# Depthwise matrices and products in 101 instead of 112 lanes, ones in one lane, and two first loads of matrices at the MLP's strips 6 and 12

## The reference, cut to what matters

```python
h = jnp.einsum('oc,bchw->bohw', w1, x)              # 48 -> 288 channels
h = relu(bn(h, g1, b1, m1, v1))
h = conv3x3_depthwise(h, wd, padding=1)             # 288 groups
h = relu(bn(h, gd, bd, md, vd))
h = jnp.einsum('oc,bchw->bohw', w2, h)              # 288 -> 48 channels
return x + bn(h, g2, b2, m2, v2)
```

## Time and profile before

| what | us |
|---|---|
| median of three runs | 2052.09 (2045.63 to 2053.95) |
| the profiled execution's own time | 2046.83 |
| its span | 2044.9 |

### The profile page before, as it was taken

The page is one execution under the profiler, slowest core; times in us unless marked ns, Lnnn a source line. Parts: engine busy times, 40 slices in busy tenths (PEclk is TensorE's granted clock), DMA queues, the critical chain, the costliest instruction groups (busy, mean ns, idle before and its releaser), DMA issues.

```text
span 2044.9 us, 76366 instructions
## 1 busy us (share of the span) xinstructions
PE 1939.0 (95%) x29704; PEld 1598.8 (78%) x29704; DVE 1447.2 (71%) x2586; ACT 1369.1 (67%) x2838; POOL 648.0 (32%) x869
## 2 busy tenths in 40 slices
PE   6999999999999996799999999999999899999998
PEld 4888888888888884455555798888888898888987
DVE  5999999999999995455556556556556556565554
ACT  2787878877778874466666566656656566666655
POOL 4333333333333325013000432525234333425230
PEclk9999999999999997899999999999999999999999
DMA  2222222222222225666554435536263545455341
GB/s 65 72 75 71 75 75 73 75 75 75 75 75 75 75 68 124 150 141 157 136 135 111 102 82 137 100 90 150 72 128 95 114 106 117 87 136 102 98 99 33
DMA packets 286441, 199.46 MB, mean 98 GB/s; under 512 B 225991, under 2 KB 275672, under 8 KB 276488
## 3 DMA queue, kind: packets, MB, share of 16 engines
q1 hardware_dynamic: 282114, 189.12, 37.3%
q0 software_dynamic: 2368, 6.98, 1.9%
q10 hardware_dynamic: 1750, 0.39, 0.1%
HBM read 129.10 MB, written 54.72 MB: 90 GB/s over the span
## 4 chain that ended last, share of the span: by engine, by line
PE 56%; ACT 2%; DMA 1%; issue 1%; DVE 1%; ACTq 0%
PE psum L1091 13%; PE psum L1110 13%; PE psum L1136 10%; PE psum L670 6%; PE psum L655 6%; PE psum L1145 5%; PE psum L644 3%; ACT h2T L1191 1%; DMA room<-tok_mid 1%; DVE h L870 1%; ACT room L736 0%; DVE room L870 0%; ACT room L740 0%; ACTq L722 0%; DMA room<-in_fc_wT 0%
## 5 line engine op out<-in xcount | busy, mean ns | idle before, releaser
L919 POOL TENSOR_TENSOR mats<-mats,dscale 112x2048 f32<-112x2048 f32 x72 | 260.9, 3624 | 455.9 <-DMA mats<-in_taps 453.1
L1091 PE MATMUL psum<-ew,xp 64*100 64x96 f32 x6144 | 318.5, 252 | 24.0 <-DVE h L870 11.2
L1191 ACT ACTIVATE h2T<-psum 96x1024 f32<-96x1024 f32 x192 | 195.9, 1021 | 198.3 <-PE psum L1145 198.3
L870 DVE TENSOR_SCALAR h<-psum 100x384 f32<-100x384 f32 x384 | 212.1, 557 | 155.7 <-PE psum L1091 134.8
L1091 PEld LDWEIGHTS psum<-ew,xp 64*100 64x100 f32 x6144 | 291.3, 165 | 33.6 <-DVE h L870 14.1
L1110 PE MATMUL psum<-h,mats 112*64 112x128 f32 x4608 | 269.3, 276 | 6.6 <-issue 5.0
L1110 PEld LDWEIGHTS psum<-h,mats 112*64 112x64 f32 x4608 | 253.6, 138 | 15.5 <-issue 6.3
L869 ACT ACTIVATE room<-psum 64x512 f32<-64x512 f32 (+1 forms) x384 | 206.6, 538 | 84.6 <-PE psum L1110 78.1
L343 PE MATMUL psum<-kb,qa 128*64 128x256 f32 x2048 | 253.2, 383 | 1.0 <-DVE prob L437 0.5
L870 DVE TENSOR_SCALAR room<-psum 64x512 f32<-64x512 f32 (+1 forms) x288 | 174.2, 605 | 71.7 <-PE psum L1110 65.7
L1136 PE MATMUL psum<-h2T,pw 128*64 128x128 f32 x3072 | 211.1, 280 | 11.3 <-ACT h2T L1191 9.5
(11 more groups left out here) (152 smaller groups left out, 3245.9 us busy)
## 6 DMA issues: line engine op xcount, KB each, us to landing
mats<-in_taps SPq DMA_DIRECT2D x69, 896.0 KB, 6.7
tok_mid<-mid SPq DMA_DIRECT2D x128, 224.0 KB, 1.9
room<-tok_mid SPq DMA_DIRECT2D x64, 448.0 KB, 3.8
piece<-img_mid SPq DMA_DIRECT2D x196, 63.8 KB, 2.4
img_mid<-room SPq DMA_DIRECT2D x128, 97.5 KB, 2.9
kb<-kk SPq DMA_DIRECT2D x512, 24.0 KB
out<-yc SPq DMA_DIRECT2D x32, 384.0 KB, 4.5
scratch<-in_x_tokens SPq DMA_DIRECT2D x126, 96.0 KB, 2.0
```

Of the source, the lines that this page charges most:

```text
L870: return nc.vector.tensor_scalar(dst, src, 0.0, None, ALU.max)
L919: nc.gpsimd.tensor_tensor(m, m, bc(scale[0:MROWS, at:at + TCH], 2, POUT), ALU.mult).then_inc(mats_scaled, 1)
L1091: mm = nc.tensor.matmul(ring[(j + u) % 4][0:PIN, p:4 * CH:4], xp[hx][rows, 2 * j + p, :], w1[rows, c, :], start=True, stop=True)
L1191: nc.scalar.activation(h2T[n % 2][0:CH, :, :], turned_at(n, last)[0:CH, :, 0:POUT * PART], ACT.Copy).then_inc(copied, 1)
```

## The change

MROWS becomes PIN + 1 = 101: the matrices in DRAM, their loads, their scaling, the products of L1110 and the batch norm's tiles `dn` lose the lanes 101 to 111. The ones are loaded from one row into lane 100 of `h1` instead of from sixteen broadcast rows into lanes 96 to 111. The first loads of `mats[0]` and `mats[1]` move behind the clearing of `yc`, and GpSimd waits before each: until strip 6 and until strip 12 of the MLP are done.

```diff
-MROWS = 112
+MROWS = PIN + 1
@@
-            loads += [(h1[CH:MROWS, :, :].rearrange("q c n -> q (c n)"), d["ones"].partition_broadcast(MROWS - CH))]
+            loads += [(h1[PIN:MROWS, :, :].rearrange("q c n -> q (c n)"), d["ones"])]
             assert len(loads) == 25
             for dst, src in loads:
                 pool.dma_start(dst, src).then_inc(w_loaded, 16)
-            for s in range(LOADS - 1):
-                pool.dma_start(mats[s][0:MROWS, :, :], d["taps"][s]).then_inc(mats_begun[s], 16)
             nc.gpsimd.memset(y[:, 0:H // 2, :], 0.0).then_inc(y_stored[0], 32)
             pool.wait_ge(y_stored[0], 32)
             nc.gpsimd.memset(y[:, H // 2:H - PH, :], 0.0).then_inc(y_done, 1)
             pool.wait_ge(y_done, 1)
             nc.gpsimd.memset(y[:, H - PH:H, :], 0.0).then_inc(y_stored[1], 32)
             pool.wait_ge(y_stored[1], 32)
+            for s in range(LOADS - 1):
+                pool.wait_ge(mlp_done, 6 * (s + 1))
+                pool.dma_start(mats[s][0:MROWS, :, :], d["taps"][s]).then_inc(mats_begun[s], 16)
             for s in range(2):
                 pool.wait_ge(img_stored[s], 32 * (H // WS // 2))
@@
-        "ones": np.ones(CH * PATCHES, np.float32),
+        "ones": np.ones((1, CH * PATCHES), np.float32),
```

## The result

The changed kernel takes 3511.39 us in the median (3510.52 to 3514.43, four runs), the kernel before 2051.68 in the same runs: 1.716 times as long, 95% interval 1.711 to 1.720. The forecast was 3570 us, its range 3400 to 3950.

What follows compares the result with a forecast made beforehand. TensorE was taken to bound the kernel before, matrix loads on one DMA engine after. 1151.9 - 16 + 1.5 + 2201 + 168 + 27 + 34 = 3567; + 2 = 3570 us, range 3400 to 3950.

Steps and rivals of the forecast that it cites:

- the MLP's start: Start of the MLP: TensorE's 13.89 us idle and the cold stretch after it go, some 16 us saved.
- the line empty over the cuts: Middle chunk of 7 halves: the one engine has no matrices to load while GpSimd cuts pieces, 24 us each, 168 us.
- from the last landing to the end: Kernel's end: scaling, the last two units' 26.1 us and 3 us for a low clock, 34 us together.
- the 98 packets left for the 97 rows: Transfers at the kernel's start: 530 packets less 432 leave 98, so 97 rows, a prime, used one engine; so would 101.
- T: Time of one 101-row load of matrices on one DMA engine: 827,392 bytes at 25.9 GB/s, 31.9 us.
- Rival B: SP's matrix loads: one engine, but at the burst's 16.4 GB/s, 50.5 us a load, 4853 us in all; chance 0.10.
- Rival C: SP's matrix loads: split rounds up, 7 rows on 14 engines, all hidden, 2031 us, faster; chance 0.07.
- Rival D: SP's matrix loads: one engine each, different from load to load, three side by side, 2330 us; chance 0.08.
- the moved loads would disturb the MLP: MLP strips: the two moved first loads might stall it, 14 us each at worst; taken as 0, kept 0 to 28.
- the cover: Convolution chunks: TensorE's 36 us hide under 96 us of loads on one engine, even at half clock.
- L1110's duration unchanged: Sign in the convolution: products and scaling keep their own durations with 101 lanes; L1110 was at 276 ns.
- the landing time: Sign on SP's queue: median landing of the matrices some 32 us or a multiple, not 6.7.

## Why the prediction was right, and where it was off

By its own terms, in us:

| term | predicted | measured in after |
|---|---|---|
| the MLP's start | 16 | 16.5 (1151.85 to 1135.38) |
| 69 loads | 69 x 31.9 = 2201 | 69 x 31.20 = 2153 |
| the line empty over the cuts | 7 x 24 = 168 | 161, seven intervals of 53.4 to 55.0 less 31.2, and 0.3 before each |
| stores in the line | 27 | 26, seven intervals of 34.85 less 31.2 |
| from the last landing to the end | 34 | 31.3 from the scaling at 3477.21 to the end at 3508.5, and about 1 before it |

**The step that decided** was the 98 packets left for the 97 rows, read as "one engine, because 97 is a prime". The runs of 101, 102, 104, 105, 106 and 115 rows bear it out with 1, 6, 13, 15, 2 and 5 engines. The Trainium skill ("DMA: Bandwidth & Descriptors", section "Why a DMA increments its semaphore by 16 and not by 1") has the rule in this form, and all six agree with it; its exception for GpSimd's queue agrees, too, with the 128 packets above.

**The term that was mis-sized** was T, 31.9 against 31.20 us, 48 of the 59 us between forecast and result. I took the rate of a window in which all engines were busy, 25.9 GB/s; an engine alone does 26.5. The same skill page's section "Specifications" gives about 27 GiB/s for one engine. That is 29.0 GB/s, and T by it an estimate of 28.5 us; the engine alone did 26.5 GB/s here, so the measurement decides. The other terms were off by 11 us together, nearly all to the same side.

**Rival B** (the burst's slow rate is an engine's own) fell: alone, the engine is quick, and the table above shows the slow rate only when thirteen or more work. **Rival C** (rounding up) fell for SP's queue and holds for GpSimd's. **Rival D** (another engine from load to load) fell: three loads in flight would have landed side by side, and they land 31.19 us apart. That the moved loads would disturb the MLP was kept as 0 to 28 us, and was about 0: TensorE waits 2.0 us in all from 820 to 1110 us.

**Right about the cover:** the products in 101 lanes, the scaling and TensorE's whole 36 us a chunk lay under the line of loads; the first shows best in the run with 112 loaded rows. What I had put wrongly is the sign to look for: "L1110's duration unchanged". It grew from 276 to 359 ns in the mean, because TensorE begins each pair of units after some 25 us of idleness at 1.2 GHz (the granted clock is 0.50 from 3480.88 to 3483.00). That lay under the line as well and cost only the last units: 5.52 us for 64 matmuls of L1111 at the end, where the whole last stretch of 68 took 4.00.

```profile
3480.88 5.52 PE L1111 MATMUL psum<-h,mats 101*64 101x128 f32 x64 [25.44 <-POOL mats L919]
```

The other sign that failed is the landing time: the profile has none for SP's loads of 101 rows, and its chain of waits puts their time down to "another core or an unknown queue" (33% of the span). Whoever reads only the chain doesn't find the cause; GpSimd's waits and the packet counts show it.

## What to carry to other kernels

Before changing how many rows a DMA of SP has, count its completion packets in a profile, and take a row count whose largest divisor up to 16 is what you want: a transfer of 101 rows is 10% smaller than one of 112 and takes 31.2 us instead of 6.7. A transfer that has time need not use all engines: 102 rows on six were hidden as well as 112 on sixteen, and took 0.7% less of the kernel's time (2017.4 against 2032.3 us). And when a hidden load becomes the bound, look at what else its issuer's queue waits for: the exchange of pieces, free before, cost 160 us.

## What the runs showed of the hardware that was not expected

Thirteen engines at once did worse than fifteen or sixteen, 14.3 GB/s for one against 18.5 and 16.4, and 10 us more for the kernel than with 112 rows (ratio 0.998 against 0.993); 102 rows on six ran at 24.4. Whether it is where the 8 rows of each engine lie in DRAM or in the lanes stays open.

SP itself is held while loads wait for the one engine. In after the issue of a load of matrices takes this long (min/median/max ns), where it was 312/313/1706 before:

```profile
L1052 SPq DMA_DIRECT2D mats<-in_taps x69: 251/15469/38960, 1135.4 to 3393.6; - x69
```

That the engine's queue is full then is my reading; no row shows its depth. It cost nothing that shows, as all that SP had to issue stood behind the loads in the same queue anyway.

The split into 96 and 5 rows was 6 us faster than 112 rows at once, with as much idle time by issue (17.1 us against 16.8). In the trace of 112 rows a pause of 2.69 us is followed by slow products, in that of the split one of 2.57 us is not:

```profile
1586.04 12.21 PE L1112 MATMUL psum<-h,mats 101*64 101x128 f32 x160 [2.69 <-issue]
...
1581.14 8.97 PE L1112 MATMUL psum<-h,mats 101*64 101x128 f32 x160 [2.57 <-issue]
```

The granted clock was 0.73 in the window of the first (1586 to 1598.5) and 1.00 in that of the second (1581 to 1591), and the 3.2 us between the two stretches are half of the 6. Why nearly equal pauses end so differently stays open.
